# A two-block network on one core: stack loads with sixteen as the outer dimension, another order ahead of the scan, and products of ones in TensorE's waits

## What is computed

```python
mod = silu(c) @ wmod                       # six rows of 512 per block: sa, ca, ga, sb, cb, gb
h = layernorm(x) * (1 + ca) + sa
# block 0, first half: a selective scan over the 1024 tokens
xp = h @ x_proj_w.T                        # 16 columns dt_in, 16 columns B, 16 columns C
dt = softplus(dt_in @ dt_proj_w.T + dt_proj_b)
for t in tokens:                           # state (512, 16)
    s = exp(dt[t] * A) * s + dt[t] * B[t] * h[t]
    y[t] = s @ C[t] + D * h[t]
x = x + ga * y
# block 0, second half: a linear layer plus eight low-rank experts, weighted by a router
# block 1, first half: causal attention, 32 heads of 16, ALiBi slopes, softmax
# block 1, second half: a gated layer (512 to 1376 and back) with truncation to integers
```

## Time and profile before

| | us |
|---|---|
| median of three runs | 941.78 |
| the runs | 938.93, 941.78, 942.89 |
| the profiled execution, its own time | 939.05 |
| span of that execution, first to last instruction | 937.2 |
| TensorE busy | 855.5 (91%) |
| VectorE busy | 762.1 (81%) |
| ScalarE busy | 439.2 (47%) |
| GpSimd busy | 262.6 (28%) |

### The profile page before, as it was taken

One profiled execution on the slowest core, in us unless ns is written; L12 is line 12 of the kernel. 1 busy time (PEld: TensorE's weight loads), 2 busy tenths in 40 slices (PEclk: granted clock), 3 DMA queues, 4 the chain that ended last, 5 costly groups with the idle time before them and its releaser, 6 DMA issues.

```text
span 937.2 us, 12092 instructions
## 1 busy us (share of the span) xinstructions
PE 855.5 (91%) x4165; PEld 410.1 (44%) x4165; DVE 762.1 (81%) x1624; ACT 439.2 (47%) x828; POOL 262.6 (28%) x213
## 2 busy tenths in 40 slices
PE   3787978899978998799999999999999999999996
PEld 2334524454427453344444444444434444444442
DVE  6589999999996876598899989998245799776776
ACT  2667655656652031100666666667541656433100
POOL 1047899999994000031000000000001334000000
PEclk8689799999999999899999999999999999999999
DMA  9200060300006006820552255310015000000001
GB/s 347 94 1 0 1 269 1 134 1 1 0 1 201 0 29 151 197 69 1 87 78 47 34 77 78 53 29 1 2 39 202 1 0 0 1 0 1 12 34 46
DMA packets 27238, 54.34 MB, mean 58 GB/s; under 512 B 5876, under 2 KB 12660, under 8 KB 25896
## 3 DMA queue, kind: packets, MB, share of 16 engines
q1 hardware_dynamic: 27176, 53.56, 21.7%
HBM read 44.96 MB, written 8.39 MB: 57 GB/s over the span
## 4 chain that ended last, share of the span: by engine, by line
PE 62%; DVE 6%; DMA 1%; POOL 1%; SPq 1%; ACT 1%; issue 0%; POOLq 0%
PE ps L1135 16%; PE ps L997 7%; PE ps L1146 6%; PE ps L979 6%; PE ps L1019 5%; PE ps L963 4%; PE ps L966 3%; PE ps L1056 3%; PE ps L908 3%; PE ps L1036 3%; PE ps L982 2%; DVE ps L1403 1%; PE ps L747 1%; PE ps L902 1%; DMA stack<-in_alibi 1%; PE ps L911 1%
## 5 line engine op out<-in xcount | busy, mean ns | idle before, releaser
L700 ACT ACTIVATE prob<-ps 128x512 f32<-128x512 f32 x288 | 160.1, 599 | 124.4 <-PE ps L982 96.2
L468 POOL TENSOR_TENSOR hC<-hs,C_sb 128x512 f32<-128x512 f32 x128 | 162.1, 1283 | 59.3 <-DVE hs L1288 51.3
L889 PE MATMUL ps<-hC,identf 128*128 128x512 f32 x256 | 136.1, 634 | 24.1 <-POOL hC L468 22.9
L979 PE MATMUL ps<-stack 123*128 123x512 bf16 (+3 forms) x384 | 113.8, 327 | 0.2
L636 ACT ACTIVATE ps<-dtT,nA 128x512 f32<-128x512 f32 x128 | 88.2, 689 | 47.5 <-DVE hs L1288 47.5
L424 POOL TENSOR_TENSOR rstd<-veps,mhalf 128x4 f32<-128x4 f32 x8 | 8.1, 1012 | 358.4 <-DVE veps L1173 358.4
L1410 DVE TENSOR_REDUCE mrow<-ps 128x1 f32<-128x512 f32 x128 | 82.0, 683 | 11.4 <-PE ps L966 11.2
L889 PEld LDWEIGHTS ps<-hC,identf 128*128 128x128 f32 x256 | 44.0, 194 | 90.0 <-POOL hC L468 77.3
L997 PE MATMUL ps<-prob,V 128*32 128x512 f32 (+3 forms) x768 | 81.6, 498 | 0.7 <-ACT prob L700 0.7
L1135 PE MATMUL ps<-hT,wg 128*128 128x512 f32 (+1 forms) x176 | 79.1, 592 | 0.0
L1135 PE MATMUL ps<-hT,wu 128*128 128x512 f32 (+1 forms) x176 | 79.1, 592 | 0.0
(11 more groups left out here) (194 smaller groups left out, 1334.1 us busy)
## 6 DMA issues: line engine op xcount, KB each, us to landing
stack<-parts_dram SPq DMA_DIRECT2D x96, 128.0 KB
wmod<-in_wmod SPq DMA_DIRECT2D x4, 1536.0 KB, 11.3
parts_dram<-qkp SPq DMA_DIRECT2D x16, 384.0 KB, 2.7
wmod<-in_wmod SPq DMA_DIRECT2D x4, 1024.0 KB, 9.8
wattn<-in_wattn SPq DMA_DIRECT2D x1, 3072.0 KB, 10.0
wg<-in_wg SPq DMA_DIRECT2D x1, 2752.0 KB, 12.3
wu<-in_wu SPq DMA_DIRECT2D x1, 2752.0 KB, 10.5
wd<-in_wd SPq DMA_DIRECT2D x1, 2560.0 KB, 11.4
```

The lines of the kernel that those rows point to most:

```text
L468: pool.tensor_tensor(hC[:, c, :], hs[:, c, :], C_sb[:, m % 2, :], ALU.mult).then_inc(S["hc_done"], 1)
L700: A_(prob[:, u % 4, j, :], ps[:, 3 + F % 3, :], ACT.Exp).then_inc(S["exp_done"], 1)
L889: mm(ps[:, c, :], identf[:], hC[:, c, :], start=False, stop=(s == NS - 1), skip_group_check=True).then_inc(S["sum_done"], 1)
L979: ins = mm(ps[:, bank, col:col + w], qk[0:ATT_ALL, 1, j, tile(kb)], qk[0:ATT_ALL, 0, j, q0:q0 + w], start=True, stop=not diag)
```

## The change

It has two parts.

*Stack loads.* The columns of the q and k weights, and their bias, are reordered on the host so that the rows of a group come feature first and head second. The four rows of one feature are then contiguous in `parts_dram`, 8 KB. A stack is filled by six loads of parts in place of twelve: 48 rows, 32 rows and 16 rows, once for q and once for k. The outer dimension of each source is the sixteen features of a head; the part comes next. A k part that is needed several times is read with a stride of zero. The position rows come from a host array in the order in which they land. `load_stack(0)` stands behind the write of block 4 and `load_stack(1)` behind that of block 6. `S_QK` is 9 in place of 8, so the first scores come one block later.

*The order ahead of the scan.* The bias of dt becomes a seventeenth row of the weight `dtw`, against a row of ones in `dtin`; one small load goes. ScalarE normalises token tiles 1 to 3 (subtract, then scale), VectorE only tile 0, after its first step on `wmod`. In the softplus "plus one" goes from ScalarE to VectorE (`plus`), `arguments` goes, and its maximum is taken in the final sum straight from PSUM. The B product of state 0 goes ahead of `x_proj(1)`; the B and C products of state 1 and the four `y_start` are placed among the first state's sums. `decay` of tiles 0 to 2 of state 0 is moved up between ScalarE's copies. `keep_states` keeps two columns at once. Two small blocks are moved inside the scan (the gate `ga` from state 4 to 15 on VectorE, `dgA` from states 12 to 15 to states 17 to 20 on ScalarE). `busy` issues bfloat16 products of a tile of ones, 256 columns each, that nobody reads: 20 before the first transposes, 8 after `mod_cols`, 5 after each `x_proj`, and 20 before the B product of state 0. The router's wait becomes one per feature tile.

```diff
-S_QK = 8
+S_QK = 9
...
             def load_stack(g):
-                for o, order in ((0, PARTS_Q), (1, PARTS_K)):
-                    for b, part in enumerate(order):
-                        at_ = o * D + g * GH * HD
-                        load(stack[g % 3][16 * b:16 * b + 16, o, :, :],
-                             parts_dram[part, at_:at_ + GH * HD, :].rearrange("(h d) t -> d h t", d=HD), stk[g % 3])
-                load(stack[g % 3][ATT_K:ATT_S, 1, :, :].bitcast(U16),
-                     a["alibi"][g * GH:(g + 1) * GH, :, :].rearrange("h r t -> r h t"), stk[g % 3])
+                for first, count in ((0, 3), (3, 2), (5, 1)):
+                    at_ = g * GH * HD
+                    q = parts_dram[0:count, at_:at_ + GH * HD, :].rearrange("q (d h) t -> d q (h t)", h=GH)
+                    load(stack[g % 3][16 * first:16 * (first + count), 0, :, :], q, stk[g % 3])
+                    at_, part = D + g * GH * HD, 3 - count
+                    k = parts_dram[part:part + 1, at_:at_ + GH * HD, :].rearrange("q (d h) t -> d q (h t)", h=GH)                         .to_broadcast([HD, count, GH * T])
+                    load(stack[g % 3][16 * first:16 * (first + count), 1, :, :], k, stk[g % 3])
+                load(stack[g % 3][ATT_K:ATT_S, 1, :, :].bitcast(U16), a["alibi"][g], stk[g % 3])

             for i, (ob, h) in enumerate(QK_ORDER):
                 sp.wait_ge(S["qk_split"], i + 1)
                 sp.dma_start(parts_dram[:, ob * P:(ob + 1) * P, half(h)].rearrange("q p t -> p q t"), qkp[:, i % 3, :, :]) \
                   .then_inc(qk_wr[i % 3], 16)
-                if i == 5:
+                if i == 4:
                     for r in range(3):
                         sp.wait_ge(qk_wr[r], 16 * (2 if r < 2 else 1))
                     load_stack(0)
-                if i == 7:
+                if i == 6:
...
+            pool.memset(dtin[:], 1.0).then_inc(S["setup"], 1)
...
+            act.wait_ge(S["nm"], 1)
+            for t in range(1, 4):
+                A_(xn0[:, t, :], x_tok[:, t, :], ACT.Identity, bias=nmean[:, t:t + 1]).then_inc(S["cent"], 1)
+            act.wait_ge(S["ln_rstd"], 1)
+            act.wait_ge(S["ln_norm"], 1)
+            for t in range(1, 4):
+                act.wait_ge(S["cent"], t)
+                A_(xn0[:, t, :], xn0[:, t, :], ACT.Copy, scale=rstd[:, t:t + 1]).then_inc(S["ln_norm"], 1)
+
+            act.wait_ge(S["in_misc"], 16 * 5)
...
+            def magnitude(c):
+                act.wait_ge(S["dt_mm"], c + 1)
+                A_(sp_log[:, c, :], ps[:, 4 + c, :], ACT.Abs).then_inc(S["sp_a"], 1)
+
             def soft(c):
-                src = ps[:, 4 + c, :]
-                act.wait_ge(S["dt_mm"], c + 1)
-                A_(sp_log[:, c, :], src, ACT.Abs, bias=dtb[:, c:c + 1]).then_inc(S["sp_a"], 1)
                 act.wait_ge(S["sp_a"], c + 1)
-                link(A_(sp_exp[:, c, :], sp_log[:, c, :], ACT.Exp, scale=-1.0))
-                A_(sp_w[:, c, :], sp_exp[:, c, :], ACT.Copy, bias=1.0).then_inc(S["sp_w"], 1)
+                A_(sp_exp[:, c, :], sp_log[:, c, :], ACT.Exp, scale=-1.0).then_inc(S["sp_x"], 1)
+                act.wait_ge(S["sp_x"], c + 1)
                 A_(uT[:, c, half(0)], sp_exp[:, c, :], ACT.Square, scale=SQRT_HALF).then_inc(S["sp_e"], 1)
                 act.wait_ge(S["sp_w"], c + 1)
                 A_(sp_log[:, c, :], sp_w[:, c, :], ACT.Ln).then_inc(S["sp_ln"], 1)

-            for part in range(3):
-                bc_part(0, part)
-            for c in range(DC - 1):
+            bc_part(0, 0)
+            magnitude(0)
+            bc_part(0, 1)
+            soft(0)
+            bc_part(0, 2)
+            for c in range(1, DC - 1):
+                magnitude(c)
                 soft(c)
             ln_out(0, 0, 0, 1, (1,))
+            magnitude(DC - 1)
             soft(DC - 1)

             def z_out(c):
                 act.wait_ge(S["dt_mm"], DC + (c if c else DC))
-                A_(dtT[:, c, half(1)], ps[:, c, :], ACT.Identity, bias=dtb[:, c:c + 1]).then_inc(S["sp_z"], 1)
-
+                A_(dtT[:, c, half(1)], ps[:, c, :], ACT.Copy).then_inc(S["sp_z"], 1)
+
+            def keep_states(m, c):
+                act.wait_ge(S["scan_done"], m * DC + c + 2)
+                at_ = state[:].rearrange("p (c s) -> p c s", s=NS)
+                A_(at_[:, c:c + 2, m:m + 1], hs[:, c:c + 2, HALF - 1:HALF], ACT.Copy).then_inc(S["st_done"], 2)
+
+            def decay(i):
+                m, c = i // DC, i % DC
+                h, s = m // NS, m % NS
+                if m == 0:
+                    act.wait_ge(S["sp_u"], c + 1)
+                    act.wait_ge(S["sp_rd"], 3 + c if c < 2 else DC)
+                if m == NS:
+                    act.wait_ge(S["sp_pu"], c + 1)
+                if i >= 2:
+                    act.wait_ge(S["scan_done"], i - 1)
+                A_(ps[:, DA_BANK + c % 2, :], dtT[:, c, half(h)], ACT.Exp,
+                   scale=nA[:, c * NS + s:c * NS + s + 1]).then_inc(S["da_done"], 1)
+                if c % 2 and 0 <= i - 3 < NS * DC:
+                    keep_states((i - 3) // DC, (i - 3) % DC)
+
+            act.wait_ge(S["negA"], 2)
+            decay(0)
...
             act.wait_ge(S["xp_mm"], 2)
             act.wait_ge(S["dt_mm"], DC)
-            A_(dtin[:], ps[0:RANK, 0, :], ACT.Copy).then_inc(S["xp_in"], 1)
+            A_(dtin[0:RANK, :], ps[0:RANK, 0, :], ACT.Copy).then_inc(S["xp_in"], 1)
             bc_part(1, 0)
+            decay(1)
             z_out(1)
             bc_part(1, 1)
             z_out(2)
             bc_part(1, 2)
-            act.wait_ge(S["negA"], 2)
+            decay(2)
...
+                    if m or c == 3:
+                        decay(m * DC + c)
...
+            def busy(count, bank):
+                flat = ones[:].bitcast(BF16)
+                for _i in range(count):
+                    mm(ps[:, bank, 0:2 * P], flat[:, 0:P], flat, start=True, stop=True)
+
+            pe.wait_ge(S["setup"], 2)
+            pe.wait_ge(S["in_x0"], 16)
+            busy(20, 1)
             pe.wait_ge(S["in_id"], 16)
             ln_transpose(0, 0)
-            pe.wait_ge(S["setup"], 1)
             pe.wait_ge(S["mod_acc"], 1)
             mod_cols((0, 1), 0).then_inc(S["mod_mm"], 1)
+            busy(8, 1)
...
+            def broadcast_b(m):
+                h, s = m // NS, m % NS
+                if s == 0:
+                    pe.wait_ge(S["xp_bc"], h + 1)
+                if m == 0:
+                    pe.wait_ge(S["sp_rd"], 2)
+                    pe.wait_ge(S["sp_a"], 2)
+                else:
+                    pe.wait_ge(S["dbx_done"], dbx_count(m - 1, DC - 1 if m <= NS else DC - 2))
+                    if m > NS:
+                        pe.wait_ge(S["b_evac"], m - NS)
+                mm(ps[:, B_BANK, :], sel[:, s:s + 1].to_broadcast([96, P]), BCs[:, half(h)],
+                   start=True, stop=True).then_inc(S["b_mm"], 1)
+
+            def broadcast_c(m):
+                h, s = m // NS, m % NS
+                if m:
+                    pe.wait_ge(S["c_evac"], m)
+                if m <= NS:
+                    slot_read(m - 1)
+                elif m - 2 >= NS:
+                    slot_read(m - 2)
+                mm(ps[:, C_BANK, :], sel[:, s + NS:s + NS + 1].to_broadcast([96, P]), BCs[:, half(h)],
+                   start=True, stop=True).then_inc(S["c_mm"], 1)
+
+            def broadcast(m):
+                broadcast_b(m)
+                broadcast_c(m)
...
             x_proj(0)
-            pe.wait_ge(S["in_misc"], 16 * 6)
+            busy(5, 1)
+            pe.wait_ge(S["in_misc"], 16 * 5)
             pe.wait_ge(S["xp_in"], 1)
             dt_proj(0, 0)
             bc_rest(0, 0)
             dt_proj(0, 1)
+            dt_proj(0, 2)
             bc_rest(0, 1)
-            dt_proj(0, 2)
             dt_proj(0, 3)
             pe.wait_ge(S["xp_bc"], 1)
             ln_transpose(0, 1)
+            pe.wait_ge(S["sp_a"], 1)
+            pe.wait_ge(S["sp_rd"], 1)
+            busy(20, C_BANK)
+            broadcast_b(0)
             x_proj(1)
+            busy(5, 2)
...
-            broadcast(0)
+            broadcast_c(0)
             pe.wait_ge(S["xp_in"], 2)
             dt_proj(1, 1)
...
-            for c in range(DC):
-                y_start(0, c)
             for m in range(N_ALL):
                 h, s = m // NS, m % NS
                 for c in range(DC):
                     if c == 0 and m in SLOTS and m < NS or c == 2 and m in SLOTS and m >= NS:
                         slot(m)
-                    if c == 0 and m + 1 < N_ALL and m != NS:
+                    if c == 0 and 0 < m and m + 1 < N_ALL and m != NS:
                         broadcast(m + 1)
+                    if m == 0:
+                        y_start(0, c)
                     if c == DC - 1 and m == N_ALL - 1:
                         pe.wait_ge(S["scan_done"], N_ALL * DC)
                         pe.wait_ge(S["c_evac"], N_ALL)
...
```

(43 more changed lines are left out.)

88 lines of the change are left out of this document (23 added, 65 removed).

## The result

The changed kernel takes 937.0 us (median of 20 runs, 934.5 to 940.8) against 941.7 (20 runs of the kernel before, 938.9 to 945.4): a ratio of 0.996, 95% interval 0.9949 to 0.997. So the change is worth 4.7 us where 17.5 were forecast, and 937.0 lies outside the range of 918 to 930. The interval leaves out 1, so the small gain is real; by the bound of 0.5% it is still the case "same". Its profiled execution took 934.45 us (span 932.7), 4.5 us less in span than the one of before.

A forecast was written before the change was run, and what follows sets the result against it. VectorE was taken to bound the scan, TensorE the part from the router on. Gains of 9.3 + 3.4 + 2.2 + 1.1 = 16.0 us took the profiled 939.05 to 923.0, stated as a median of 924.3; range 918 to 930.

The forecast's parts named there:

- What bounded the kernel, and the two places: VectorE bounds the scan, TensorE the router onward; the change targets waits in the first 61 us and 371 to 380.
- Landing of the stack: First stack, before the first scores: 8 us of transfer, landing at 373.3, needed at 374.6, so the 8.3 us stall goes.
- slow bound: First stack's transfer staying at 141 GB/s: it lands at 377.4 and 2.8 us of stall stay.
- What is late next: q and k blocks: writes 5 to 7 behind loads are covered; one moved score costs 0.4 us, leaving 9.3 gained.
- a wait that eats the gain: Anywhere in the kernel: an unseen wait takes the whole gain; chance 0.02.
- Up to the first projection: Start of the kernel to the end of the first `x_proj`: 3.4 us gained (2.6 to 4.4).
- Up to the second state: From the first projection to VectorE's first product of state 1: 2.2 us gained, last `z_out` 27.7 after the projection.
- The scan: Inside the scan: the moved blocks cost VectorE the same elsewhere or sit on engines with room; nothing gained or lost.
- The router: First half of the router: three products run while the fourth feature tile is written; 1.1 us gained, at least 0.5.
- Loads no faster: Stack loads stay at 141 GB/s and TensorE waits 2.8 us more; 928 us in all, chance 0.13.
- the front gives little: Ahead of the scan and in the router: 4.1 us gained instead of 6.7, or less; 927 to 930, chance 0.13.
- Fewer DMA engines: Merged stack loads each run on 3, 2 or 1 DMA engines; stack lands at 395, 945.6 us, chance 0.04.

The follow-up runs named there:

- ring5: The changed kernel with five buffers instead of three for the split parts of q and k; 929.9 us, ratio 0.989.
- mod_first: The changed kernel with ScalarE's shift and scale copies and first half of `hT` ahead of its wait for small loads and `dgD`; 936.9 us.
- b_only: The changed kernel with the stack part taken back, leaving the rest of the change; 940.6 us, ratio 0.9995.
- after_old: The changed kernel with `ga` and `dgA` back at their old places in the scan; 936.5 us, ratio 0.9963.
- b_old: `b_only` with `ga` and `dgA` back at their old places in the scan; median 939.9 us, ratio 1.0009.
- ring5_late1_z: `ring5` with `load_stack(1)` behind the write of block 12 and ScalarE's second `decay` behind its B and C parts and copies; 929.4 us.

## Why the prediction was wrong

**What bounded the kernel, and the two places**: right. Behind the first product of the attention before and after take the same time, 488.5 and 488.6 us.

**Landing of the stack** (8 us of transfer): mis-sized. In the time frame of before, to which 3.6 us are added here, the loads start at 363.3, forecast 363.8; the stack lands at 376.5, forecast 373.3; and it is needed at 374.8, forecast 374.6. So place and need were right, and issue and transfer take 13.2 us instead of 9.5. Hence 1.7 us of stall, near the 2.8 of the slow bound. The middle of the bounds was too fast a choice, the more so as 48 and 32 partitions are, in its own words, "nearer to sixteen than to 128": all engines were busy at 141 GB/s already, and 174 came out on average.

**What is late next** (0.4 us): this is the step that failed. The prediction saw that writes 5 to 7 stand behind loads, named write 7, the split of block 10 and 383 us, and called it "covered by about two blocks". It left out that block 8 must wait for write 5. It put write 7 too early: in the time frame of before it was done at 389.5 us. And it counted the cover for the copies of q and k, not for VectorE's other work: the splits stand in one list with `negT` and the reductions of the scores. While a split waits, no maximum is taken, no PSUM buffer comes free, and TensorE stands in front of the next scores. The two waits, 12.2 us on VectorE, cost TensorE 6.4 us with the clock, by `ring5`, and the wait put down to the moved score came to about 1 us (1.73 against 0.78) and not 0.4. So this part brought 1.1 us in the profile instead of 9.3. A new wait on the late writes was listed among what would show the prediction wrong; among the chances, a wait that eats the gain had 2 in 100.

**Up to the first projection** (3.4 us): 1.5. Less than even the slow end: `mod_cols` took 2.57 us, since the clock fell inside it, and `dgD` started at 17.81, before at 16.99, though there was one small load fewer; so `hT` starts 0.7 us later than forecast, and `x_proj` took 5.34 us, like before: about 3.5 of them at the low clock, and the end at the full one. It was reckoned at 5.2 for the slow end and 3.5 for the fast one. The clock at this place isn't the same in each profile: in `mod_first` `x_proj` took 4.8 us, in `ring5` 6.06.

**Up to the second state** (2.2 us): the last `uT` comes 22.4 us behind the projection's end, forecast 22.7. What failed is the last `z_out`, forecast 27.7 behind it. `y_start` waits for that copy, which ended 28.7 behind: the copies stand behind `decay(1)`, which waited 1.74 us for VectorE, and four products ran at the low clock (3.78 us). The rest of the order did as laid out: from `y_start` to VectorE's first product of state 1 it was 3.9 us, against 6.2 before and 3.8 forecast. The gain at state 1 is 2.4 us in all, where 5.6 were forecast.

**The scan** ("nothing" for the moved blocks): failed. It took 1.4 us more than before in this profile and 4.8 in `b_only`'s. Of these 1.0 are the case that the prediction named and left out of its sum, that the three postponed `y_start` push the B product of state 2 back; the trace fits it, and no run tests it. The rest, 0.4 and 3.9, goes in the profiles when the moved blocks are put back; in the medians of `after_old` and `b_old` that can't be told from nothing.

**The router** (1.1 us): larger, 2.0 between state 31 and the router's first product, and 0.6 more up to the first q and k product. The 2.0 are the wait by feature tile: the router's first product comes 0.9 us behind the start of `hT`, before 2.9. TensorE had no long wait in front of the router, and ran at the full clock (1.00, before 0.72): 26 records in 3.45 us, 0.13 each, against 0.18 for each record of the earlier trace rows (32 in 5.82). That the shorter wait is what kept the clock up is likely, and not shown.

**The rivals.** "Loads no faster" happened in part: the stack came in 13.2 us and not 15.1, but 1.7 of its 2.8 us of stall stayed; "the front gives little" happened and went further than its 4.1 us. Both together would have been 931; the missing 6 us are the late writes. "Fewer DMA engines" is refuted: the DMA share stayed at 0.93 to 1.25 with the merged loads.

## What to carry to other kernels

Before a load is moved ahead of writes in a queue, ask when each write behind it comes back, which buffer that holds, and what else stands in the list of the engine that waits for the buffer. Here 12.2 us of waits for two writes turned a saving of 8 us into 1, and two more buffers brought most of it back: 937.0 to 929.9 us. The trace of before held the figure that was missing: a write behind a stack's loads took 10.8 us, where one by itself took 2.5. A gain in front of a long stretch with its own pace has to be looked for at the end of that stretch, and in the medians: here the profiled run of after is over 2.5 us under its kernel's median, and that of `ring5_late1_z` 3.9 over.

## What the runs showed of the hardware

- Six loads of 48, 32 and 16 partitions moved 174 GB/s on average, twelve of 16 partitions with rows of 8 KB 120, each over four windows of 2 us, with the engines' share at or near 1 in both. Longer rows did not help the narrow loads: 16.2 us to land against 15.1 with rows of 2 KB.
- A write of 384 KB issued on the same queue behind 1.7 MB of loads took 10 us to land, one behind two such groups 17.1; with nothing ahead it took 2.5 (after, writes 5, 7 and 4).
- TensorE's clock fell to its 1.2 GHz level during sixteen float32 products of a single column, with the engine busy by the trace (after). In `ring5`, with the same list up to there, it stayed at 1.00 through them (1.95 us against 2.57). 20 and 8 bfloat16 products of ones ahead of and behind them brought nothing (937.0 us with, 935.8 without), and behind the same list `x_proj` took 5.34 us in one profile (after) and 6.06 in another (`ring5`).
- The scan repeats to 0.1 us over three profiles where nothing ahead of it is changed (210.6, 210.7, 210.7), and its states 8 to 31 do so too with the new order, as long as the two blocks stand at their old places. With the blocks moved it took 212.0 to 216.9.
- The 488.5 us behind the first product of the attention repeat to 0.1 us in eleven profiles; in seven the granted clock is about 0.7 in the first 5 us, and 1.4 to 1.7 us are lost there.
